# Layer 2's attention with half 1 normed beside the values, its query copies on ScalarE, and four other moves

## The reference, cut to what matters

```python
xn = (x - mu) * jax.lax.rsqrt(var + LN_EPS) * gamma + beta     # a second norm: x is normed already
qkv = xn @ w_qkv                                               # 192 -> 3 * 768
q, k, v = jnp.split(qkv, 3, axis=-1)                           # 12 heads of 64
dots = jnp.einsum('bhid,bhjd->bhij', q, k) * scale
attn = jax.nn.softmax(dots, axis=-1)                           # the block mask hides nothing at n = 36
out = jnp.einsum('bhij,bhjd->bhid', attn, v)
return out.transpose(0, 2, 1, 3).reshape(b, n, HEADS * DIM_HEAD) @ w_out + b_out
```

```python
h = h + _L1_attn_ref(_layernorm(h), ...)     # "grid" in the kernel
h = h + _L1_ffn_ref(_layernorm(h), ...)      # an attention too: A1
h = h + _L2_attn_ref(_layernorm(h), ...)     # A2
h = h + _L2_ffn_ref(_layernorm(h), ...)      # experts with a router: M2 (layer 0 has M0, layer 3 M3)
```

## Time and profile before

| | |
|---|---|
| median of 3 runs | 730.83 us (730.2 to 731.36) |
| the profiled execution | 730.98 us |
| its span, first to last instruction | 729.2 us |
| mean granted TensorE clock | 0.981 of 2.4 GHz |
| busy in the span | PE 684.4 (94%), DVE 494.4 (68%), ACT 358.7 (49%), POOL 165.7 (23%) |
| chain that ended last | PE 73%, DVE 13%, ACT 7%, issue 5%, DMA 1%, POOL 1% |
| A1 | about 260 to 372 us of the span |
| A2 | about 372 to 461 us |

### The profile page before, as it was taken

One profiled execution on the slowest core, in us unless ns is written; L12 is line 12 of the kernel. 1 busy time (PEld: TensorE's weight loads), 2 busy tenths in 40 slices (PEclk: granted clock), 3 DMA queues, 4 the chain that ended last, 5 costly groups with the idle time before them and its releaser, 6 DMA issues.

```text
span 729.2 us, 16235 instructions
## 1 busy us (share of the span) xinstructions
PE 684.4 (94%) x6345; PEld 621.8 (85%) x6345; DVE 494.4 (68%) x1216; ACT 358.7 (49%) x833; POOL 165.7 (23%) x164
## 2 busy tenths in 40 slices
PE   6999999999999999999896999999999999999996
PEld 6789798999988777898786998889999977789986
DVE  3658478888877954788635674578675756666784
ACT  0366455555543233688431442455545548457652
POOL 1200036444261022343102000026443320000000
PEclk9999999999999999999897899999999999999999
DMA  9922022222221000111000010032230300112000
GB/s 256 273 65 82 2 59 80 81 80 80 70 78 45 1 0 1 46 45 45 2 1 1 1 46 2 1 104 60 61 119 18 97 1 2 53 51 80 23 22 25
DMA packets 16891, 39.40 MB, mean 54 GB/s; under 512 B 3692, under 2 KB 4684, under 8 KB 16623
## 3 DMA queue, kind: packets, MB, share of 16 engines
q1 hardware_dynamic: 14840, 37.29, 17.8%
q10 hardware_dynamic: 1976, 1.08, 0.6%
HBM read 37.90 MB, written 0.44 MB: 53 GB/s over the span
## 4 chain that ended last, share of the span: by engine, by line
PE 73%; DVE 13%; ACT 7%; issue 5%; DMA 1%; POOL 1%; POOLq 0%; ACTq 0%; DVEq 0%; SPq 0%
PE PS L864 6%; PE PS L806 6%; PE PS L731 5%; PE PS L611 4%; PE PS L740 4%; PE PS L615 4%; PE PS L613 4%; PE PS L614 4%; PE PS L612 4%; PE PS L663 3%; PE PS L827 3%; DVE AL L1601 2%; PE PS L664 2%; PE PS L665 2%; PE PS L667 2%
## 5 line engine op out<-in xcount | busy, mean ns | idle before, releaser
L1064 ACT ACTIVATE MIX<-PS 128x288 f32<-128x288 f32 x118 | 48.5, 411 | 114.7 <-PE PS L615 114.5
L611 PE MATMUL PS<-XH,WH 128*128 128x288 f32 x284 | 86.3, 304 | 3.5 <-DVE OT L1590 1.4
L613 PE MATMUL PS<-XH,WL 128*128 128x288 f32 x284 | 83.7, 295 | 0.0
L614 PE MATMUL PS<-X,WH 128*128 128x288 f32 x284 | 83.7, 295 | 0.0
L612 PE MATMUL PS<-XL,WH 128*128 128x288 f32 x284 | 83.7, 295 | 0.0
L615 PE MATMUL PS<-X,WL 128*128 128x288 f32 x284 | 83.6, 294 | 0.0
L1927 POOL TENSOR_TENSOR rstd<-var,nhalf 96x3 f32<-96x3 f32 x18 | 16.6, 921 | 289.2 <-DVE var L1338 289.2
L1590 DVE TENSOR_TENSOR OT<-MIX,PS 128x288 f32<-128x288 f32 x94 | 42.3, 451 | 39.0 <-ACT MIX L1064 38.3
L1601 DVE TENSOR_TENSOR AL<-OT,AH 128x288 fp32r<-128x288 f32 x118 | 59.0, 508 | 3.3 <-ACT AH L1078 2.3
L1444 DVE TENSOR_TENSOR WL<-RG,WH 128x768 fp32r<-128x768 f32 (+2 forms) x46 | 57.8, 1259 | 3.5 <-ACT WH L1044 3.3
L663 PE MATMUL PS<-AH,DW 128*128 128x288 f32 x166 | 52.7, 318 | 7.2 <-DVE AL L1601 7.0
(11 more groups left out here) (255 smaller groups left out, 1719.6 us busy)
## 6 DMA issues: line engine op xcount, KB each, us to landing
RG<-in_gu_l0f_dram SPq DMA_DIRECT2D x8, 512.0 KB, 4.9
RG<-in_gu_l0f_dram SPq DMA_DIRECT2D x16, 256.0 KB, 5.8
RG<-in_gu_l2f_dram SPq DMA_DIRECT2D x9, 384.0 KB, 3.7
RG<-in_gu_l2f_dram SPq DMA_DIRECT2D x18, 192.0 KB, 4.4
RD<-in_wd_l0f_dram SPq DMA_DIRECT2D x8, 384.0 KB, 3.2
RD<-in_wd_l2f_dram SPq DMA_DIRECT2D x9, 288.0 KB, 2.8
RD<-in_wd_l3f_dram SPq DMA_DIRECT2D x6, 384.0 KB, 3.2
BIG<-in_patch_dram SPq DMA_DIRECT2D x6, 288.0 KB, 7.7
```

What stands on the lines that cost most here:

```text
L611: mm(o, WH[r][:, 0, w], XH[:, cols], start=True, stop=False)
L613: mm(o, WL[r][:, 0, w], XH[:, cols], start=False, stop=False)
L614: mm(o, WH[r][:, 1, w], X1[:, cols], start=False, stop=False)
```

## The change

1. The norm of A2's half 1 is done on VectorE ahead of its loop, all three parts in a row, with the two weight splits between them. TensorE turns half 1 in step 0, behind `qk(0)`; `x2_high` and `evac_xt` of half 1 move from step 4 to step 1, and the values of half 1 from steps 5 to 7 to steps 2 to 4.
2. A2's query copies move from VectorE to ScalarE, behind the key copy of the same unit.
3. In the tails of A1 and A2, the exponential of the last unit (unit 11) is put behind `probs_turned(9)` and `outs(8)` on ScalarE.
4. In all three experts stages the second of the two sum copies of each half moves from ScalarE to VectorE (`second_sum`, semaphore f2_sb). Half 0's stands behind VectorE's last `low`, and half 1's between the next stage's statistics and its norm.

```diff
 def pieces(a, i):
     n = 4 if a.tm else 3
-    i -= 4 if a is A2 else 0
+    i -= 1 if a is A2 else 0
...
# TensorE
                 def by_tokens(j):
-                    pe.wait_ge(S["f_sb"], 4 * mi + 2 * j + 2)
+                    pe.wait_ge(S["f_sb"], 2 * mi + j + 1)
+                    pe.wait_ge(S["f2_sb"], 2 * mi + j + 1)
...
-                    if a is A2 and i == 3:
-                        turn(stage, 1)
                     for p in pieces(a, i):
                         values(1, p)
                     if 0 <= i - lag < a.units:
                         qk(i - lag)
+                    if a is A2 and i == 0:
+                        turn(stage, 1)
# ScalarE
                 for j in range(2):
                     act.wait_ge(S["w3_done"], u0 + m.half_end(j))
-                    for part in range(2):
-                        activation(summed(m, j, part), FB(j, part), ACT.Copy).then_inc(S["f_sb"], 1)
+                    activation(summed(m, j, 0), FB(j, 0), ACT.Copy).then_inc(S["f_sb"], 1)
...
+                        elif a is A2:
+                            o, i = q_views(a, u, h)
+                            last = activation(o, i, ACT.Copy, scale=mh[:, 3 + h:4 + h])
...
-                    if a is A2 and i == 4:
+                    if a is A2 and i == 1:
                         x2_high(stage, 1)
...
                         keys(i - lag)
-                        if a is not A2:
-                            queries(i - lag)
-                    if 0 <= i - lag - 1 < a.units:
+                        queries(i - lag)
+                    tail = a.ng == 6 and i >= a.units + lag
+                    if not tail and 0 <= i - lag - 1 < a.units:
                         exps(i - lag - 1)
                     if 0 <= i - lag - 3 < a.units:
                         probs_turned(i - lag - 3)
                     if 0 <= i - lag - 4 < a.units:
                         outs(i - lag - 4)
+                    if tail and 0 <= i - lag - 1 < a.units:
+                        exps(i - lag - 1)
# VectorE
+            def second_sum(m, j):
+                dve.wait_ge(S["w3_done"], MU0[m.name] + m.half_end(j))
+                V.tensor_copy(summed(m, j, 1), FB(j, 1)).then_inc(S["f2_sb"], 1)
...
                 if 2 in parts:
+                    if j == 0 and k and STAGES[k - 1][0] == "moe":
+                        second_sum(STAGES[k - 1][1], 1)
                     normalised(n, src, j).then_inc(S["ln_normed"], 1)
...
                     evac_xt(k, kind, a, 0)
+                for part in range(3):
+                    layer_norm(k, 1, (part,))
+                    if a is A2 and part < 2:
+                        w2_split(4 + part)
                 if a is A2:
                     return
-                layer_norm(k, 1)
...
-                    if a is A2 and i == 0:
-                        layer_norm(stage, 1, (0,))
-                    if a is A2 and i == 4:
+                    if a is A2 and i == 1:
                         evac_xt(stage, "attn", a, 1)
...
-                    if a is A2 and 0 <= i - lag < a.units:
-                        queries(i - lag)
...
-                    if a is A2 and i in (1, 2):
-                        layer_norm(stage, 1, (i,))
-                    if a is A2 and i < 2:
-                        w2_split(4 + i)
```

More of the change, by code:

```diff
@@ L396, in bass_vit_tower @@
             "gu_hi", "gu_lo", "dn_hi", "dn_lo",
-            "comb_made", "ct_ready", "ct_sb", "cb_ready", "cb_sb0", "cb_sb1", "f_sb", "ysum_ready",
+            "comb_made", "ct_ready", "ct_sb", "cb_ready", "cb_sb0", "cb_sb1", "f_sb", "f2_sb", "ysum_ready",
             "grid_ready", "grid_sb", "grid_s", "grid_e", "grid_o", "grid_turned", "grid_osb",
@@ L1173, in queries @@
                     U = u0 + u
-                    if u == 0:
+                    if u == 0 and a in PADDED:
                         act.wait_ge(S["pads"], PADDED.index(a) + 1)
@@ L1746, in mean_square @@
                     V.tensor_scalar(ssq[:, 1, :], ssq[:, 0, :], 1.0 / 64, EPS, ALU.mult, ALU.add).then_inc(S["tm_sum"], 1)
[L1748 to L1756, removed]
                 def shift(u):
@@ L1877, in _ @@
             for i, (kind, arg) in enumerate(STAGES):
+                if i and STAGES[i - 1][0] == "moe":
+                    second_sum(STAGES[i - 1][1], 0)
                 if i == 0 or STAGES[i - 1][0] != "attn":
@@ L1887, in _ @@
             for j in range(2):
+                second_sum(M3, j)
                 stream(len(STAGES), j)
```

## The result

Four runs of the changed kernel took 716.98, 719.2, 719.62 and 728.13 us, with a median of 719.41; the four of the kernel before beside them had a median of 731.03 us. The ratio is 0.983, with a 95% interval of 0.981 to 0.986. The forecast was 716.6 us, with a range of 712.0 to 721.5. By the medians the gain is 11.6 us, where 14.2 was forecast. That the profiled execution is within 0.4 us of the forecast is partly luck: it is the fastest of the four, with a mean granted clock of 0.993, and the next two had 0.988 and took 2.2 and 2.6 us more.

The account below looks back on a forecast made before the run. TensorE, busy 94% of the span, bounds the kernel; only its waits and halved clock pay. Terms -12.1 + 0 - 1.35 - 0.9 - 0.8 + 0.73 + 0.15 = -14.3 took 730.98 to 716.7; forecast 716.6 us, range 712.0 to 721.5.

Parts of the forecast that it names:

- Part 1: A2's opening: half 1's norm ready 0.3 us early, waits and halved clock gone, 12.1 us won (6.3 less 3, to 12.8).
- rebuilt 31.5: A2's opening: TensorE's time from the end of `qk(0)` to step 7's end, 31.5 us instead of 43.6.
- Part 2: A2's query copies on ScalarE: covered with slack 0.4 us, cost 0; bounds 0 to 5.5.
- Part 3: Tails of A1 and A2: output matmuls start 1.35 and 0.9 us earlier, plus 0.8 less halved clock.
- A1 keeps its halved clock, A2's goes half the time: Tails: of 1.5 us of halved clock in either, half of one is won, 0.8; bounds 0 and 3.0.
- just what A2 has now: A1's tail: gaps shrink from 2.7 to 1.6 us, A2's gap before the change, where the clock fell too.
- Part 4: Sum copies on VectorE: +0.73 us in M0, 0 in M2, +0.4 in M3, -0.25 at the end; bounds -0.3 to +2.5.
- B: A2's opening: half 1's norm late by 1 to 3 us, some clock lost again; 718 to 723, say 720; chance 0.13.
- C: A2: TensorE waits for ScalarE, 0.3 to 0.5 us in each of eleven units; 721 us; chance 0.08.
- D: A2's steady units: late query pair leaves gaps, clock stays at 1.2 GHz; slower, about 750 us; chance 0.03.
- gap near 1 us: A2's steady units: the gap per unit from which the slower, half-clock case of about 750 us decides.
- A: Tails of A1 and A2 keep full clock and the opening's waits vanish: 713.7 us; chance 0.16.

Follow-up runs that it names:

- again: The changed kernel, nothing altered, in a later set of six runs: median 718.42 us, ratio 0.977 to the kernel before.
- late: The changed kernel with half 1's statistics taken twice more ahead of the last normalised: median 718.1 us, ratio 0.979.
- p1: The kernel before with the early norm and turn of A2's half 1 alone, query copies still on VectorE: median 721.37 us, ratio 0.982.
- p12: The kernel before with half 1's early norm and turn and A2's query copies on ScalarE: median 721.26 us, ratio 0.982.
- p2: The kernel before with A2's query copies on ScalarE alone: median 734.03 us, ratio 1.000.
- p3: The kernel before with only the order of ScalarE's last copies in the tails of A1 and A2 changed: median 728.46 us, ratio 0.994.
- no4: The changed kernel with all sum copies back on ScalarE: median 714.42 us, ratio 0.975.
- end_only: The changed kernel with the sum copies back on ScalarE, all but the last, in M3's last half: median 714.14 us, ratio 0.975.
- tails: The changed kernel with idle turns of the constants on TensorE ahead of the output products in the three tails: median 716.2 us, ratio 0.978.

## Why the prediction was right

**The number.** Medians gave 11.6 us of the 14.2 forecast. The three runs that count agree in span less clock loss (709.4, 708.9 and 709.3 us) and differ in clock loss (5.0, 8.6 and 8.6): what came out otherwise than forecast is the clock. In "again" the same kernel gained 14.3 us by the medians, so four runs do not settle the size to better than some 3 us.

**Part 1** was right in mechanism and size: 12.5 us in the traces against 12.1 forecast, 31.1 us of TensorE against the rebuilt 31.5. The norm was ready 0.3 us early, as forecast, and "late" shows that this margin is real and so small that a delay over 0.37 us passes straight on to TensorE. Both powers took 1.49 us with a weight split beside them, as the earlier trace rows had it for half 0; that is in line with the exclusion in the Trainium skill, "SBUF — State Buffer", section "Who interferes with whom", and the sum had counted it. The copies of half 1's values cost 0.33 and 0.28 (0.25 was taken).

By the means of p1, part 1 gave 6.4 us of rest and 5.4 of clock, 11.8 together, and p12 the same (6.5 and 5.3); by the median losses, 13.9 before and 10.1 in both, the clock's share is 3.8. The halved stretch in the opening alone was 6.8 us of loss, so some of it seems to come back at other places: that the halved clock of the opening is won for good was a little too simple. All parts together lowered the loss by 8.2 and the rest by 7.5; singly, the rests add up to the same within their errors (p1 6.4, p3 2.2, the sum copies -0.6: 8.0). What inside part 1 gave how much (the early norm, the earlier turn, the earlier values) no run separates; "late" tests the norm alone.

**Part 2** at nothing: right (p12 against p1 0.1 us, p2 alone 1.000). The pair of query copies took 0.89 us, less than the 1.05 of A1's pair that was counted; from the changed kernel's timeline of ScalarE:

```profile
380.50 0.89 ACT L1184 ACTIVATE QB<-PS,mh 128x288 f32<-128x288 f32 x2
```

**Part 3**: the waits were right, 1.37 and 0.82 against 1.35 and 0.9, and 2.2 us in p3's rest. The step "A1 keeps its halved clock, A2's goes half the time" was mis-sized for the profiled run (3.3 against 0.8), and not meaningful for a single tail: the same wait of 1.10 us came with 2.89 us of output matmuls in one execution of the same kernel and 5.44 in another. Nor does p3 bear it out as a mean: its mean loss is 2.0 us lower, but its median loss of 13.8 is before's 13.9, whose mean a few runs of 19 to 24 us raise. Two readings in this part were off. By its own terms A1's gaps shrink from 2.72 to 1.37 us, not to 1.6 (measured 0.19 + 1.10 = 1.29), so "just what A2 has now" did not hold. And sixteen output matmuls at full clock take 2.89 us, not 3.0, so a halved tail costs 1.6 to 1.7.

**Part 4** was right as a loss: +1.1 us in the traces against 0.9, and 0.6 to 0.9 in the rest of no4 and end_only. Only the copy at the very end pays.

**The rivals.** B and C did not come: no turn waited for XN, no unit for QB. D was far off. Its "gap near 1 us", from which the clock would be lost, is no limit that rows give: behind the 1.04 us of the earlier trace rows the clock stayed full to 392 us, and behind 0.95 us in A1 it fell in twelve of thirteen profiles. A named the two full-clock tails that the profiled run has, but priced nothing at A3, which took the 3.3 us back.

## What to carry to other kernels

Work whose input is ready long before its turn should be issued there, in front of the engine's paced work: half 1's two variances were 14.0 us apart (374.82 to 388.81 in the earlier trace rows) with unit work between them, and 4.0 us apart (372.99 to 377.00) when done in a row. When a trace shows a halved clock, don't book the whole stretch as won: compare the sum of such stretches over several executions, and price waits apart from them. A wait on TensorE that comes before work which is ready (M3's turned sums before the next down units) is mended by changing the order of TensorE itself, and that paid more here (1.9 us) than moving the copy to another engine (0.17 at the very end, a loss elsewhere).

## What the runs showed of the hardware

In the profiles, read per microsecond, the halved stretches were about 3.4 or 6.8 us long, with a loss of 1.7 or 3.4 us (one of 14 us in the kernel before). The same kernel had them at the tails of A1 and A2 in one execution and at the end of A3 in another, with the same waits to 0.01 us. One, in tails, came behind 8 us in which TensorE was never idle for more than 0.19 us (part of its work there was the transposes put in). The Trainium skill, "TensorE: Matmul & The Clock Gate", section "A second HAM failure mode: psum-queue depth-cycling", says of another kernel (bf16, 512 columns) that short idles between groups of matmuls, if frequent, make the clock swing. The attention stages with many small matmuls and frequent bank changes might fit that, but filling three of the idles with transposes changed the mean loss by nothing that six runs can tell (6.9 against 7.1). What decides when it falls stays open.

One execution of p2 took 1631.27 us. In its page the matmuls of L611 take 574 ns on average, where "again" has 304, and the other groups of that shape 565 to 570; the granted clock is recorded as 1.00, and ScalarE's and VectorE's instructions last as always. I have no cause for it. The rows, p2 first and then again:

```profile
L611 PE MATMUL PS<-XH,WH 128*128 128x288 f32 x284 | 162.9, 574 | 0.0
```

```profile
L611 PE MATMUL PS<-XH,WH 128*128 128x288 f32 x284 | 86.3, 304 | 3.5 <-DVE OT L1605 1.4
```
